# Attention products between the blocks of a feed-forward layer: three places become two

## The reference

```python
scores = jnp.einsum('bhtd,bhsd->bhts', q, k) * (1.0 / np.sqrt(DH))
s_mat = scores * d_mat                      # d_mat: exponential decay, causal
denom = jnp.maximum(jnp.abs(jnp.sum(s_mat, axis=-1, keepdims=True)), jnp.exp(-m)) + BACKEND_EPS
h = jnp.einsum('bhts,bhsd->bhtd', s_mat, v) / denom
...
h = jax.nn.silu(_tlin(x, w1_w, w1_s)) * _tlin(x, w2_w, w2_s)
h = jax.nn.gelu(_tlin(h, h1_w, h1_s), approximate=False)
h = jax.nn.gelu(_tlin(h, h2_w, h2_s), approximate=False)
return _tlin(h, w3_w, w3_s)
```

## Time and profile before

| | |
|---|---|
| median of 3 runs | 764.75 us (764.41 to 764.94) |
| the profiled execution | 764.41 us |
| its span, first to last instruction | 762.7 us |
| TensorE busy | 754.7 us (99%) |
| VectorE busy | 543.6 us (71%) |
| ScalarE busy | 384.1 us (50%) |
| GpSimd busy | 53.7 us (7%) |
| mean granted TensorE clock | 0.999 |

### The profile page before, as it was taken

How to read it: one execution, slowest core, us unless ns; L and a number is a source line. 1 busy time by engine, 2 the same in 40 slices (tenths; PEclk the granted TensorE clock), 3 DMA queues, 4 the chain that set the end, 5 groups by cost and what they waited for, 6 DMA issues and landing times.

```text
span 762.7 us, 15214 instructions
## 1 busy us (share of the span) xinstructions
PE 754.7 (99%) x6296; PEld 631.7 (83%) x6296; DVE 543.6 (71%) x1295; ACT 384.1 (50%) x577; POOL 53.7 (7%) x67
## 2 busy tenths in 40 slices
PE   8999999999999999999999999999999999999998
PEld 4778888888898888988888888888889888898887
DVE  6788786696957868588676877658695784965554
ACT  3566456463365634556454554646335562445332
POOL 3400020000100020000200002000020000000000
PEclk9999999999999999999999999999999999999999
DMA  9393112200022000310005001230102100540640
GB/s 327 98 426 110 35 52 88 108 29 30 29 112 83 29 31 28 140 56 29 31 29 193 0 31 39 87 127 23 37 29 112 55 1 3 172 160 11 177 144 30
DMA packets 14617, 63.46 MB, mean 83 GB/s; under 512 B 2016, under 2 KB 2896, under 8 KB 11728
## 3 DMA queue, kind: packets, MB, share of 16 engines
q1 hardware_dynamic: 12960, 50.12, 18.9%
q0 software_dynamic: 1296, 11.53, 3.9%
q10 hardware_dynamic: 288, 0.79, 0.3%
HBM read 53.94 MB, written 8.50 MB: 82 GB/s over the span
## 4 chain that ended last, share of the span: by engine, by line
PE 94%; DVE 1%; ACT 0%; issue 0%
PE ps_f L1601 31%; PE ps_f L1602 30%; PE ps_f L1566 8%; PE ps_f L1567 8%; PE ps_f L1641 4%; PE ps_f L1642 4%; PE ps_a L1506 2%; PE ps_a L1489 2%; PE ps_a L1341 1%; PE ps_a L1539 1%; PE ps_a L1462 1%; PE ps_a L1455 1%; PE ps_a L1498 0%; PE ps_f L1576 0%; DVE stats L1063 0%; DVE z L1050 0%
## 5 line engine op out<-in xcount | busy, mean ns | idle before, releaser
L1601 PE MATMUL ps_f<-h_hi,wgt 128*128 128x512 f32 x1024 | 401.5, 392 | 0.0
L1602 PE MATMUL ps_f<-h_lo,wgt 128*128 128x512 f32 x1024 | 398.7, 389 | 0.0
L1601 PEld LDWEIGHTS ps_f<-h_hi,wgt 128*128 128x128 f32 x1024 | 192.2, 188 | 40.5
L1602 PEld LDWEIGHTS ps_f<-h_lo,wgt 128*128 128x128 f32 x1024 | 192.3, 188 | 39.0
L752 ACT ACTIVATE work<-ps_f,scl 128x512 f32<-128x512 f32 x128 | 87.5, 684 | 164.9 <-PE ps_f L1602 164.3
L1169 DVE TENSOR_TENSOR h_lo<-work,h_hi 128x512 fp32r<-128x512 f32 x128 | 86.6, 690 | 101.7 <-ACT h_hi L757 100.6
L1566 PE MATMUL ps_f<-h_hi,wgt 128*128 128x512 f32 x252 | 99.1, 393 | 0.0
L1567 PE MATMUL ps_f<-h_lo,wgt 128*128 128x512 f32 x252 | 98.3, 390 | 0.0
L739 ACT ACTIVATE work<-ps_f,scl 128x512 f32<-128x512 f32 x64 | 44.2, 690 | 88.2 <-PE ps_f L1567 87.5
L757 ACT ACTIVATE h_hi<-work 128x512 fp32r<-128x512 f32 x128 | 81.0, 633 | 4.1
L1160 DVE SCALAR_TENSOR_TENSOR work<-ps_f,scl,work 128x512 f32<-128x512 f32 x64 | 48.1, 751 | 39.4 <-PE ps_f L1567 37.9
(11 more groups left out here) (214 smaller groups left out, 685.2 us busy)
## 6 DMA issues: line engine op xcount, KB each, us to landing
decay<-m_rows SPq DMA_DIRECT2D x14, 1024.0 KB, 6.6
decay<-w_cols SPq DMA_DIRECT2D x22, 512.0 KB, 4.2
wgt<-w_cols POOLq DMA_DIRECT2D x5, 1024.0 KB, 11.8
v_aug<-ctx_tok SPq DMA_DIRECT2D x8, 528.0 KB, 3.9
wgt<-w_cols POOLq DMA_DIRECT2D x2, 2048.0 KB, 14.1
x_kept<-xs SPq DMA_DIRECT2D x8, 512.0 KB, 2.6
xs<-x SPq DMA_DIRECT2D x7, 512.0 KB, 3.6
ctxT<-ctx_t SPq DMA_DIRECT2D x7, 512.0 KB, 3.3
```

Of the source, the lines that this page charges most:

```text
L1601: pe.matmul(ps_f[:, bank], w, moving(h_hi[layer][:, k], as_is), start=(k == 0), stop=False)
L1602: last = pe.matmul(ps_f[:, bank], w, moving(h_lo[layer][:, k], as_is), start=False, stop=(k == KH - 1))
```

## The change

`scores(j, 1)` moves from behind block 3 to behind block 4, and both tiles of the first batch's values follow it directly. They are written to banks of `ps_f` that the network has free at that point, those of blocks 2 and 3, and block 6 has to wait until ScalarE has copied them out. `make_state`, both tiles of the second batch's values and `read_state` stand together in the middle of block 7. The place behind block 5 is empty. `take_near` is split by batch and copies both tiles, so `take_num` now adds two operands that both lie in `num` and `state`. `k_wt` moves to the half of `num` that the first batch's values do not use. On VectorE, `weigh_scores(j, 1)` and `take_state` stand later.

```diff
-        k_wt = num[:, 0:W * HEADS * DH].rearrange("p (b h d) -> p b h d", b=W, d=DH)
+        def k_wt(j):
+            at = 0 if first(j) else TILES * HEADS * DV
+            return num[:, at:at + W * HEADS * DH].rearrange("p (b h d) -> p b h d", b=W, d=DH)
...
-            return ps_a[:, 2 + b, 0:HEADS * DV]
+            if b == 0:
+                return ps_f[:, (turn_of(j - 1) + 2 + t) % 4, 0:HEADS * DV]
+            return ps_a[:, 2 + t, 0:HEADS * DV]
...
-            def take_near(j):
-                dst = num[:].rearrange("p (b t e) -> p b t e", b=W, t=TILES)[:, :, 0]
-                act.wait_ge(s_pv, Q * j + W)
-                act.activation(dst, ps_a[:, 2:4, 0:HEADS * DV], ACT.Copy).then_inc(s_near, 1)
+            def take_near(j, b):
+                act.wait_ge(s_pv, Q * j + TILES * (b + 1))
+                for t in range(TILES):
+                    last = act.activation(num[:].rearrange("p (b t e) -> p b t e", b=W, t=TILES)[:, b, t], value_out(j, b, t), ACT.Copy)
+                last.then_inc(s_near, 1)
...
-                    if a_stage and m == 5:
-                        take_near(j)
+                    if a_stage and m == 4:
+                        take_near(j, 0)
+                    if a_stage and m == 6:
+                        take_near(j, 1)
...
-                dve.wait_ge(s_pv, Q * j + Q)
+                dve.wait_ge(s_near, W * j + 1)
                 dst = num[:].rearrange("p (b t e) -> p b t e", b=W, t=TILES)[:, :, 1]
-                dve.tensor_tensor(dst, ps_a[:, 2:4, 0:HEADS * DV], state[:].rearrange("p (b n) -> p b n", b=W), ALU.add)\
+                dve.tensor_tensor(dst, dst, state[:].rearrange("p (b n) -> p b n", b=W), ALU.add)\
                    .then_inc(s_num, 1)
...
-                    if a_stage and m == 1:
+                    if a_stage and m == 3:
                         weigh_scores(j, 1)
...
-                    if a_stage and m == 5:
+                    if a_stage and m == 6:
                         take_state(j)
-                    if a_stage and m == 6:
                         take_far(j)
...
             def values(j, t, b):
-                if t == 1:
-
-                    pe.wait_ge(s_near, j + 1)
+                if b == 0:
+                    pe.wait_ge(s_v, 16 * j + 16)
+                    pe.wait_ge(s_gelu, 2 * KH * (j - 1) + 3 + t)
...
-                    if a_stage and m == 3:
+                    if a_stage and m == 4:
                         scores(j, 1)
+                        values(j, 0, 0)
+                        values(j, 1, 0)
                     if a_stage and m == 5:
-                        make_state(j)
-                        values(j, 0, 0)
-                        values(j, 0, 1)
+                        pe.wait_ge(s_near, W * j)
...
                     if a_stage and m == 7:
+                        make_state(j)
+                        values(j, 0, 1)
+                        values(j, 1, 1)
                         read_state(j)
-                        values(j, 1, 0)
-                        values(j, 1, 1)
```

More of the change, by code:

```diff
@@ L530, in weigh_keys @@
                     w = e_cols[:, 0, 1, b * HEADS:(b + 1) * HEADS].rearrange("p (h o) -> p h o", o=1).to_broadcast([P, HEADS, DH])
-                    last = pool.tensor_tensor(k_wt[:, b], v_aug[:, b * TILES, :, 0:DH], w, ALU.mult)
+                    last = pool.tensor_tensor(k_wt(j)[:, b], v_aug[:, b * TILES, :, 0:DH], w, ALU.mult)
                 last.then_inc(s_kwt, 1)
@@ L1099, in mix_divide @@
                 total = heads[:, :, DH]
-                dve.wait_ge(s_near, j + 1)
+                dve.wait_ge(s_near, W * j + 1)
                 dve.wait_ge(s_num, j + 1)
@@ L1497, in make_state @@
                         strip = slice(h % ROWGRP * DH, (h % ROWGRP + 1) * DH)
-                        last = pe.matmul(ps_a[strip, b, h * DV:(h + 1) * DV], k_wt[:, b, h, :],
+                        last = pe.matmul(ps_a[strip, b, h * DV:(h + 1) * DV], k_wt(j)[:, b, h, :],
                                          v_aug[:, b * TILES, h, :], start=True, stop=True)
```

## The result

| | before | after |
|---|---|---|
| median of 6 runs | 764.69 us (764.41 to 765.35) | 771.75 us (769.55 to 772.90) |
| the profiled execution | 764.41 | 771.72 |
| its span | 762.7 | 769.8 |
| mean granted TensorE clock | 0.999 | 0.998 |

The ratio is 1.0085, 95% interval 1.0068 to 1.0102: the change makes the kernel slower by 0.85%, four times what the measurement can tell. The forecast was 765.5, with a range up to 767.1. It missed by 6.3 us. The runs of the changed kernel also lie further apart: the two shortest, 769.55 and 769.61, had a mean granted clock of 1.000 and 0.999, the other four, 771.72 to 772.90, one of 0.997 or 0.998.

The account below looks back on a forecast made before the run. TensorE, never without work in the loop, was taken as the bound, so time is the sum of distances between product starts. Seven times stall 0.31 less saving 0.20 gives +0.8 us on 764.41; median forecast 765.5, range 764.0 to 767.1.

Parts of the forecast that it names:

- The places: Attention products between network products: behind block 4 2.58 (+0.03), in block 7 2.65, against 5.46 before; saves 0.20 us a pair.
- Merging saves nothing: Rival: adjacent narrow forms cost as much as returning to the network, only the stall is left; 766.9 us; chance 0.10.
- The gelu wait: Block 4's first product waits for block 0's gelu: 0.18 late plus slow start 0.13, so 0.31 us a pair.
- the stall is only the wait: Rival: at block 4 only the 0.18 us wait is lost, without the slow start; 764.6 us; chance 0.08.
- no stall: Rival: block 0's gelu is early enough for block 4 and the saving is whole; -1.4, 763.3 us; chance 0.04.
- The covers: Slack by which other engines' work stays hidden from TensorE, such as 1.3 for first-batch values, 0.45 at the transposes.
- The thinnest: Cover of 0.3 us in block 7: `take_state` ends at 3.35, the reading comes up at 3.68 after block 6's last product.
- the shared port: Rival: `take_num`, now with two SBUF inputs, is held by GpSimd, delaying the transposes; about +10 us, 775; chance 0.05.
- The sum: Over seven pairs, stall 0.31 less saving 0.20: 7 x (0.31 - 0.20) = +0.8 us.
- signs of being wrong: A wait at line 1546 (for `take_state`) or at the transposes, or both places together costing more than 5.4 us.
- The third: Sign of error: the places behind block 4 and in block 7 together cost more than 5.4 us.
- The 0.20 for slower: Chance of slower by over 0.2%, mainly from merging saves nothing (0.10), shared port (0.05) and the reading waits for `take_state` (0.05).

Follow-up runs that it names:

- phase_bad: Changed kernel plus long-satisfied waits ahead of TensorE's wide products, 8 in pair 0 and 92 in each later pair: 781.71 us, ratio 1.0226.
- before_shift: Kernel before plus 48 long-satisfied waits ahead of TensorE's wide products in pair 0, none later: 766.90 us, ratio 1.0026.

## Why the prediction was wrong

By its own steps:

- *The places.* Forecast 2.58 (+0.03) and 2.65, a saving of 0.20 a pair; measured 2.63, 2.67 and 0.18, and 0.18 again from the length of a pair. Right, though in block 7 by luck: 0.09 too much for the reading against 0.12 left out for the slow start behind it. "Merging saves nothing" is excluded.
- *The gelu wait.* Forecast 0.31 a pair, seven times, with block 4 starting 0.41 late of block 3's last; measured 0.32 and 0.41. Right, and "the stall is only the wait" (0.18) and "no stall" are excluded. What it said of its origin was too short: the decays are late by 0.7 us because of GpSimd's step beside the masks, and this could be cured.
- *The covers.* None failed. The thinnest, forecast at 0.3 for `take_state`, was 0.30. `take_num` came first and GpSimd was held, and TensorE shows no wait at the transposes, so the shared port cost nothing there.
- *The sum.* +0.8 us for these terms; with supply stops taken away, 0.78 was measured between the medians, and 7 x 0.14 = 0.98 from the length of a pair.
- *What failed* is the step with which the working begins, the sentence on which the sum stands: that TensorE is never without work, so "the time is the sum of the distances between the starts of its products, and another engine matters only where it makes TensorE stop", together with "no product is added or removed, only their neighbours change". Who the neighbours are is what decides how fast instructions are used up, and a stop can also come from having no instructions. Nor did the number of instructions stay: the products did, the waits grew by 21. It cost 4.6 us of standing and 1.7 us of clock. None of the rivals had it, so the range, which was drawn from them, could not hold it. Of the signs of being wrong that it gave, two did not come: line 1546 and the transposes have no wait. The third, two places above 5.4 us together, came only in the pairs in which a stop fell into a place (2 and 5). The row `q8 instruction` stands on the page of before as well, and was not read.

The 0.20 for slower came from three cases, none of which happened; the kernel became slower by a fourth.

A page bears on it. The Trainium skill, page "Runtime: NRT & Kernel Launch", Instruction fetch mechanics, says that each engine's instructions are streamed in blocks of 16 KiB, 256 instructions each, and that the cost of a new block is mostly hidden. The size agrees with the packets of 16,384 bytes and the number 193 modulo 256 in fourteen stops. "Mostly hidden" holds for every other block of the loop, and fails in the fourteen cases, in which 297 instructions, more than a block, were used up in 1.3 to 2.8 us.

## What to carry to other kernels

When a change sets dense stretches of small instructions next to each other, or adds even a few instructions ahead of such a stretch, ask how fast the engine's instruction stream is used up; in the profile it shows as idle time put down to "issue" that comes in some repetitions of a loop and not in others. A difference under 1% between two versions can be their count of instructions and nothing of their order: shift the count of both with satisfied waits where they are hidden, and compare the best of each (here 0.85% became 765.64 against 764.97, or 0.09%). A wait that a move uncovers can be cured at its far end, here on GpSimd, two engines away from TensorE.

## What the hardware did that was not expected

- TensorE stopped for 0.5 to 2.4 us with nothing to wait for, at number 193 modulo 256 of its instructions, 14 times in 4 kernels, and went on 1.27 to 1.57 us after a packet of 16,384 bytes landed.
- The kernel before is subject to it too: 48 instructions more in its first pair cost it 2.1 us.
- After such a stop of 2.2 us the granted clock was 0.53 for 3.35 us; after one of 1.6 us it was 1.00. After two of 1.97 and 1.96 us in one run it was 0.57 and 1.00.
- The same work ended the program 2.8 us or 5.7 us after VectorE's last step, as TensorE's last product had the number 169 or 119 modulo 256; in the longer one its last instruction followed a packet by 1.40 us.
- 673 satisfied waits among wide products were free.

Left open: at which instruction the next block is asked for. With its 152 the model chose counts without a stop in the loop in four kernels of four (three of them share their counts up to pair 6), and gave the time of `phase_bad` within its bounds and that of `before_shift` 0.1 us too high. But in the loop packets also started up to 7.8 us after it, from there to the end of a stop it was 2.6 to 4.1 us over the fourteen and not 3.5 to 4.0, and no run measures the point by itself. Nor was a way tried that is robust for any count, such as fewer and larger narrow products.
